# Output projection of five chunks as three products of two-part operands, in place of the fp32 product

## The chip, the cores and the metric

The kernel runs on one core of a Trainium2 chip. The metric is the device time of one execution in microseconds (us). A core has five engines that work side by side, each through its own list of instructions in order, and wait for one another by semaphores: TensorE (PE in the profile, its weight loads PEld), VectorE (DVE), ScalarE (ACT), GpSimd (POOL) and SyncE (SP, which here issues transfers).

## The reference, cut to what matters

The input x has 4 x 1024 tokens of 256 numbers. Three sublayers follow one another: a mixture of eight experts, causal attention with 16 heads of 16, and the same mixture of experts again. What the change touches is the output projection of the attention, the line with `w_proj`:

```python
x = x + 0.5 * _L0_ffn_ref(_layernorm(x), ...)
x = x + _L0_attn_ref(_layernorm(x), ...)       # below
x = x + 0.5 * _L0_ffn_ref(_layernorm(x), ...)
...
out = jnp.einsum('bhqk,bhkd->bhqd', attn, v)
out = out.transpose(0, 2, 1, 3).reshape(b, t, d)
proj = out @ w_proj + b_proj
x = proj + resid
mu = jnp.mean(x, axis=-1, keepdims=True)
var = jnp.var(x, axis=-1, keepdims=True)
return (x - mu) * jax.lax.rsqrt(var + EPS) * ln_gamma + ln_beta
```

All of it is float32.

## The kernel before

The 4096 tokens are 8 chunks of 512, and a chunk is 4 tiles of 128 tokens. The program has three stages: the first mixture of experts with the attention's inputs (names that begin with a_), the attention (b_), and a last stage that holds the output projection, the attention's norms and the second mixture of experts (c_). The last stage of chunks 0 to 2 is begun inside the end of the attention (the functions called `lead`); from then on it runs in slots. Slot c works on chunk c for its experts, and on later chunks for what must be ready by then:

- TensorE in slot c: the projection of chunk c+2 (`project`, L798; it is left out in slot 0), the bias product, then four tiles t of four expert products n (`experts`, L761), each product being six matmuls (`pair_product`, L349) into one of four PSUM banks, the ring. Between the tiles stand the transposes of chunk c+1 (`turn`, behind tile 0), its router product (behind tile 1), the transposes of its logits (behind tile 2), and the transpose of its mask (`turn_mask`, before the last product of tile 3).
- VectorE in slot c: `add_residual(c+2)` (it adds the projection from PSUM to the residual and takes the statistics), `combine(c, t)` for the four tiles (eight operations each, two for each expert product; they free the ring's banks), between them `split_lo(c+1)`, `attended(c+3)` (L1020, attention's numerator times the inverse of its denominator, 128x1024), `ranks(c+1)` (which experts a token takes; its last operation, L986, writes the mask), and `norm(c+2)` and `scale(c+2)` before `combine(c, 3)`.
- ScalarE in slot c: copies out of PSUM, `residual(c+3)`, and behind it `spread(c+2)` (the logarithm and exponential of the norm), `mask_out(c+1)` (L576) and `norm(c+2)`.
- GpSimd adds the two halves of a combined tile (L471) and does the wide additions of the norms (L485, L491, L497, L502).

The order within each engine is the order in which the code is written; there is no scheduler. The ring lets TensorE be four products ahead of VectorE:

```python
def ring_wait(pe, c, i):
    if i >= 4:
        pe.wait_ge(q.combined, at(32 * c + 2 * (i - 3) if exists(c) else 32 * NCH))
...
    else:
        pe.wait_ge(q.combined, at(32 * (c - 1) + 2 * (13 + i)))
```

So the first product of tile 1 waits until VectorE has combined the first product of tile 0 of the same chunk, and the first product of tile 0 waits until it has combined the first product of tile 3 of the chunk before.

`values` (L782) in the first stage has the form that the change brings into the last stage: 24 matmuls of `pair_product`, 256 columns wide, of operands in the type float32r.

Of the kernel before, what the change touches and what calls it, by code (L numbers as in the profile page):

```python
# [15 lines left out]
F32 = mybir.dt.float32  # L16
# [7 lines left out]
P = 128  # L24
# [6 lines left out]
CH = 512  # L31
# [132 lines left out]
def ffn(nc, s, ctx, a, first):  # L164
# [7 lines left out]
    def sb(name, shape, dt=F32):  # L172

        nonlocal offset
        here, size = offset, int(np.prod(shape[1:])) * (2 if dt == BF16 else 4)
        offset += -(-size // 32) * 32
        return nc.alloc_sbuf_tensor_at(f"{tag}_{name}", shape, dt, offset=here)
# [3 lines left out]
    def sem(name):  # L181
        every.append(ctx.enter_context(nc.semaphore(f"{tag}_{name}")))
        return every[-1]
# [25 lines left out]
    if first:  # L209
        q.st2, q.aggr2, q.std2, q.rstd2, q.norm2 = sem("st2"), sem("aggr2"), sem("std2"), sem("rstd2"), sem("norm2")  # L210
        q.xh2_ready, q.turned2, q.hi2_ready, q.lo2_ready = sem("xh2_ready"), sem("turned2"), sem("hi2_ready"), sem("lo2_ready")
        q.v_bank, q.v_ready, q.qk_bank = sem("v_bank"), sem("v_ready"), sem("qk_bank")
        q.qk_hi, q.qk_rest, q.qk_mid, q.qk_lo = sem("qk_hi"), sem("qk_rest"), sem("qk_mid"), sem("qk_lo")
        q.stored = s.qk_stored = [sem(f"stored{j}") for j in range(4)]
    else:
        q.num_loaded0, q.num_loaded1, q.att_ready = sem("num_loaded0"), sem("num_loaded1"), sem("att_ready")
        q.proj_bank, q.resid_ready, q.resid_bias, q.xa_ready = sem("proj_bank"), sem("resid_ready"), sem("resid_bias"), sem("xa_ready")
        q.st3, q.aggr3, q.std3, q.rstd3, q.norm3 = sem("st3"), sem("aggr3"), sem("std3"), sem("rstd3"), sem("norm3")
        q.y_ready, q.scaled, q.x_shifted, q.x2_ready = sem("y_ready"), sem("scaled"), sem("x_shifted"), sem("x2_ready")
        q.written = sem("written")  # L220
# [36 lines left out]
        xt.append([sb(f"xt1{n}", [P, DK, CH], F32R) for n in range(2)])  # L257
    ybias = [sb(f"ybias{pair}", [P, 2, D]) for pair in range(2)]
    acc = [[sb(f"acc{par}{n}", [P, D]) for n in range(2)] for par in range(2)]


    if first:
# [287 lines left out]
    def scalar(act):  # L550
# [85 lines left out]
        def norm3(m):  # L636
# [2 lines left out]
            act.wait_ge(q.scaled, at(m))  # L639
            normalize(act, yn, lambda t: xa[:, t, :], lambda t, n: ln3[:, t, n:n + 1], q.y_ready)  # L640

        def slot(c, par, nth):
            if exists(c):
                bias_out(c, 0)
            if first and exists(c - 1):
                norm2(c - 1)
            if not first and exists(c + 2):
                norm3(c + 2)
            if exists(c + 1):
                split_hi(c + 1, 1 - par)  # L650
                logits_out(c + 1)
            if exists(c):
                bias_out(c, 1)
            if first and exists(c - 1):
                split2(c - 1)
            if not first and exists(c + 3):
                residual(c + 3)
            if exists(c + 2):
                spread(c + 2)
            if exists(c + 1):  # L660
                mask_out(c + 1, 1 - par)
            if exists(c + 2):
                norm(c + 2)
            if first and exists(c - 1):
                v_out(c - 1)
                for j in (0, 2):
                    qk_hi(c - 1, j)
                    qk_hi(c - 1, j + 1)
                    qk_mid(c - 1, j)
                    qk_mid(c - 1, j + 1)  # L670

        if first:
            nc.scalar.preload_act_table_set("natural_log_exp_and_others")
            act.dma_start(wr_in[:], s.w_router).then_inc(q.router_in, 16)
            act.dma_start(be_in[:], s.b_experts).then_inc(q.bias_in, 16)
            act.dma_start(s.brouter[:], s.b_router).then_inc(q.router_in, 16)
            act.dma_start(wqk_in, s.w_qk).then_inc(q.qk_in, 16)
            act.dma_start(wv_in, s.w_v).then_inc(q.v_in, 16)
            act.wait_ge(q.consts, 3)
            act.activation(unused[:], s.eps[:, 0:1], ACT.Exp)  # L680
            weights_hi((0,))
            spread(0)
            norm(0)
            weights_hi(range(1, 5))
            split_hi(0, 0)
            weights_hi(range(5, WBANKS))
            act.wait_ge(q.router_in, 2 * 16)
            act.sem_inc(q.apart, 1)
            logits_out(0)
            act.wait_ge(q.qk_in, 16)  # L690
            act.activation(s.wqk[0][:], wqk_in, ACT.Copy).then_inc(q.wqk_hi, 1)
            act.wait_ge(q.v_in, 16)
            act.activation(s.wv[0][:], wv_in, ACT.Copy).then_inc(q.wqk_hi, 1)
            mask_out(0, 0)
            spread(1)
            norm(1)
        else:
            def lead(early, block):
                if (early, block) == (1, 6):
                    act.wait_ge(a.v_copied, at(NG))  # L700
                    residual(0)
                if (early, block) == (1, 10):
                    residual(1)
                if (early, block) == (0, 1):
                    spread3(0)
                if (early, block) == (0, 5):
                    spread(0)
                if (early, block) == (0, 7):
                    split_hi(0, 0)
                    spread3(1)  # L710
                if (early, block) == (0, 9):
                    logits_out(0)

            a.scalar(act, lead)
            spread(1)
            mask_out(0, 0)
            norm(1)
# [5 lines left out]
    def tensor(pe):  # L723
# [74 lines left out]
        def project(m, par, pairs=(0, 1)):  # L798
# [3 lines left out]
            for pair in pairs:  # L802
# [4 lines left out]
                                                s.wp[:, h, :], start=(h == 0), stop=(h == DK - 1))  # L807
                last.then_inc(q.proj_bank, 1)

        def slot(c, par, nth):  # L810
            if not first and exists(c + 2) and not (isinstance(c, int) and c == 0):
                project(c + 2, par)
            if first and isinstance(c, int) and c == 0:

                experts(0, 0, 0, (0, 1))
# [92 lines left out]
    def vector(dve):  # L908
# [108 lines left out]
        def attended(m, par, nth):  # L1017
            dve.wait_ge((q.num_loaded0, q.num_loaded1)[par], at(16 * 3 * (nth + 1)))
            dve.wait_ge(q.proj_bank, at(2 * (m - 1)))
            dve.tensor_tensor(att[par][:], num[par][:], rec[par][:], ALU.mult).then_inc(q.att_ready, 1)  # L1020

        def add_both(m):
            dve.wait_ge(q.resid_bias, at(m + 1))
            dve.wait_ge(q.y_ready, at(m))
            for pair in range(2):
                dve.wait_ge(q.proj_bank, at(2 * m + pair + 1))
                dve.tensor_tensor(xa[:, 2 * pair:2 * pair + 2, :], pt[pair][:].rearrange("p (t d) -> p t d", d=D),
                                  residb[:, 2 * pair:2 * pair + 2, :], ALU.add).then_inc(q.xa_ready, 1)
# [12 lines left out]
        def slot(c, par, nth):  # L1041
# [16 lines left out]
                combine(c, par, 2)  # L1058
            if exists(c + 1):
                ranks(c + 1, 1 - par)  # L1060
            if first and exists(c - 1):
                split2(c - 1)
            if first and not exists(c):
# [26 lines left out]
        else:  # L1090
# [45 lines left out]
                    scale(1)  # L1136

            a.vector(dve, lead)
        slots(dve, slot)

    f = Signals()
# [453 lines left out]
```

## Time and profile before

| what | value |
|---|---|
| median of 3 runs | 1014.38 us (1014.06 to 1014.91) |
| the profiled execution, its own time | 1014.85 us |
| its span, first to last instruction | 1013.1 us |
| TensorE busy | 966.1 us, 95% |
| VectorE busy | 832.3 us, 82% |
| ScalarE busy | 512.1 us, 51% |
| GpSimd busy | 264.6 us, 26% |
| granted TensorE clock, mean | 0.977 |
| slots of the last stage | 783.8 to 1013.1 us of the span |

Busy time is the time in which an engine's records say that it works; TensorE's matmuls overlap in the records, so that the time between two starts says more than the length of one. Idle time stands in brackets behind a row, with what ended it.

### The profile page before, as it was taken

The page shows a single profiled execution, that of the slowest core. Times are in us where ns is not written, and L with a number is a line of the kernel's source. Part 1 is how long each engine was busy: PE and PEld are TensorE (multiplying, and loading weights), DVE is VectorE, ACT ScalarE, POOL GpSimd, SP SyncE. Part 2 cuts the span into 40 slices and gives each one's busy share as a digit, 9 for nine tenths or more (in the row PEclk, how much of TensorE's full clock was granted, in tenths as well). Part 3 has the DMA queues.
Part 4 walks back from the last instruction along what each step waited for, and adds up shares of the span by engine and source line. Part 5 has one row for each costly group of instructions (what it writes and reads, how often), then busy time and mean ns, then how long its engine had stood idle before and what let it go on. Part 6 is the DMA issues. An engine that isn't in the chain of part 4 may idle for free.

```text
span 1013.1 us, 18108 instructions
## 1 busy us (share of the span) xinstructions
PE 966.1 (95%) x5602; PEld 574.2 (57%) x5602; DVE 832.3 (82%) x2444; ACT 512.1 (51%) x1053; POOL 264.6 (26%) x289
## 2 busy tenths in 40 slices
PE   6899999999897799999999999999997999999997
PEld 5678887888664233333333333333343777777776
DVE  6677676867665899999999999999768788888775
ACT  4235434442322377777777777777775333232210
POOL 1012202221423311212122222222343553434311
PEclk9999999999996799999999999999999999999999
DMA  7201101103103412223222323223320111110001
GB/s 228 81 1 63 58 6 62 63 28 98 63 23 102 127 47 68 71 65 73 70 68 74 76 77 76 77 75 76 81 70 13 43 63 63 62 61 22 1 21 42
DMA packets 55058, 64.27 MB, mean 63 GB/s; under 512 B 13776, under 2 KB 37312, under 8 KB 54976
## 3 DMA queue, kind: packets, MB, share of 16 engines
q1 hardware_dynamic: 54384, 62.47, 21.6%
q8 instruction: 40, 0.66, 0.3%
q10 hardware_dynamic: 592, 0.80, 0.2%
q14 instruction: 42, 0.34, 0.1%
HBM read 41.30 MB, written 21.23 MB: 62 GB/s over the span
## 4 chain that ended last, share of the span: by engine, by line
PE 86%; DVE 8%; issue 2%; ACT 2%; DMA 1%; POOL 1%; DVEq 0%; SPq 0%; POOLq 0%; ACTq 0%
PE bank L354 39%; PE bank L1507 14%; PE bank L1337 14%; PE bank L1491 13%; PE bank L806 2%; PE bank L346 2%; ACT b_probs L1470 1%; DVE bank L1364 1%; DMA v_all<-L_ffn_w_experts 1%; PE bank L757 1%; DVE a_acc L1005 1%; DVE b_neg L1368 1%; DVE c_acc L1005 1%; DVE c_eq L978 1%; DVE a_st L309 1%
## 5 line engine op out<-in xcount | busy, mean ns | idle before, releaser
L1470 ACT ACTIVATE b_probs<-bank 128x512 f32<-128x512 f32 (+1 forms) x608 | 302.3, 587 | 121.0 <-PE bank L1491 120.5
L1364 DVE CUSTOM_DVE_ANT_0 bank<-bank,b_below 128x384 f32<-128x384 f32 (+3 forms) x512 | 234.9, 516 | 7.8 <-PE bank L1337 6.3
L1337 PE MATMUL bank<-b_ks,b_qs 96*128 96x512 bf16 (+3 forms) x768 | 226.3, 337 | 15.3 <-DVE b_neg L1368 5.4
L1491 PE MATMUL bank<-b_qs,b_ks 99*128 99x512 bf16 (+3 forms) x768 | 214.6, 331 | 4.5 <-ACT b_probs L1470 4.3
L354 PE MATMUL bank<-we,a_xt 128*128 128x512 f32 x768 | 190.6, 402 | 1.7 <-DVE a_acc L1005 1.7
L354 PE MATMUL bank<-we,c_xt 128*128 128x512 f32 x768 | 187.7, 399 | 0.5 <-DVE c_acc L1005 0.5
L1444 POOL TENSOR_SCALAR_AFFINE_SELECT b_probs<-b_probs 128x512 f32<-128x512 f32 x128 | 83.9, 656 | 333.7 <-ACT b_probs L1470 319.6
L1368 DVE TENSOR_REDUCE b_neg<-bank 128x1 f32<-128x512 f32 x256 | 160.6, 679 | 3.0 <-PE bank L1337 1.6
L354 PEld LDWEIGHTS bank<-we,a_xt 128*128 128x128 f32 x768 | 143.0, 191 | 30.7 <-DVE a_acc L1005 1.7
L354 PEld LDWEIGHTS bank<-we,c_xt 128*128 128x128 f32 x768 | 141.8, 188 | 31.8 <-DVE c_acc L1005 0.8
L1507 PE MATMUL bank<-b_probs,b_vs 128*32 128x512 f32 (+3 forms) x1536 | 155.7, 500 | 0.9 <-POOL b_probs L1444 0.9
L1337 PEld LDWEIGHTS bank<-b_ks,b_qs 96*128 96x128 bf16 x768 | 68.0, 98 | 124.6 <-DVE b_neg L1364 51.0
L1491 PEld LDWEIGHTS bank<-b_qs,b_ks 99*128 99x128 bf16 x768 | 66.1, 98 | 108.7 <-ACT b_probs L1470 70.6
L1005 DVE SCALAR_TENSOR_TENSOR c_acc<-bank,c_mask,c_acc 128x256 f32<-128x256 f32 x192 | 81.6, 477 | 22.8 <-PE bank L354 22.0
L1005 DVE SCALAR_TENSOR_TENSOR a_acc<-bank,a_mask,a_acc 128x256 f32<-128x256 f32 x192 | 81.2, 477 | 18.4 <-PE bank L354 17.9
L471 POOL TENSOR_TENSOR xs<-a_acc,a_acc 128x256 f32<-128x256 f32 (+1 forms) x32 | 24.9, 778 | 221.2 <-DVE a_acc L1005 221.2
L1364 DVE DVE_READ_ACCUMULATOR2_ANT b_neg<- 128x1 f32 x512 | 69.6, 136 | 0.0
L1507 PEld LDWEIGHTS bank<-b_probs,b_vs 128*32 128x32 f32 x1536 | 35.3, 109 | 56.9 <-ACT b_probs L1470 36.1
L471 POOL TENSOR_TENSOR xs<-c_acc,c_acc 128x256 f32<-128x256 f32 (+1 forms) x32 | 29.0, 906 | 100.9 <-DVE c_acc L1005 100.9
L1015 DVE TENSOR_TENSOR a_rest<-bank,a_part 128x512 f32<-128x512 f32 x32 | 22.1, 691 | 32.8 <-ACT a_part L620 28.2
L354 PE MATMUL bank<-a_xt2r,a_wqk 128*128 128x512 f32 x192 | 46.4, 397 | 0.0
L325 ACT ACTIVATE a_std<-a_mv,eps 128x4 f32<-128x4 f32 x16 | 4.8, 298 | 76.6 <-DVE a_mv L314 76.6
(133 smaller groups left out, 912.1 us busy)
## 6 DMA issues: line engine op xcount, KB each, us to landing
b_qs<-q_parts SPq DMA_DIRECT2D x96, 128.0 KB, 3.0
b_ks<-k_parts SPq DMA_DIRECT2D x96, 128.0 KB, 3.1
q_parts<-a_part SPq DMA_DIRECT2D x16, 384.0 KB, 2.7
k_parts<-a_part SPq DMA_DIRECT2D x16, 384.0 KB, 2.7
att_num<-b_oev SPq DMA_DIRECT2D x64, 64.0 KB, 2.2
c_num<-att_num SPq DMA_DIRECT2D x8, 512.0 KB
c_rec<-att_rec SPq DMA_DIRECT2D x16, 256.0 KB
out<-xs SPq DMA_DIRECT2D x8, 512.0 KB, 3.1
```

The lines of the kernel that those rows point to most:

```text
L346: last = nc.tensor.transpose(dst[h][:, t * P:(t + 1) * P], src[:, t, h * P:(h + 1) * P], s.ident[:])
L354: last = nc.tensor.matmul(out_, wa if x_moves else xa_, xa_ if x_moves else wa, start=(n == 0), stop=(n == len(steps) - 1))
L471: pool.tensor_tensor(s.xs[:, row(c, t), :].rearrange("p a d -> p (a d)"), acc[t % 2][0][:], acc[t % 2][1][:], ALU.add).then_inc(q.x_ready, 1)
L1005: dve.scalar_tensor_tensor(out=dst[:], in0=ring[n][:, i * D:(i + 1) * D], scalar=mask[par][:, t, 2 * n + i:2 * n + i + 1], in1=base, op0=A ...
L1015: dve.tensor_tensor(rest[j % 2][:], ring[j][:], part[j][:, 0, :], ALU.subtract).then_inc(q.qk_rest, 1)
L1337: last = nc.tensor.matmul(ms[bank][:, a * width:(a + 1) * width], qs[g.u][0:ROWS, c, i * P:(i + 1) * P], ks[g.u][0:ROWS, c, lo:lo + width] ...
L1364: last = dve.tensor_tensor_reduce(part, part, below[:, CH - width:CH], -1.0, 3.0e38, ALU.add, ALU.min, dst[:, a, :])
L1368: dve.tensor_reduce(dst, ms[bank][:, 0:len(heads) * width].rearrange("p (h w) -> p h w", w=width), AX.X, ALU.max, negate=True).then_inc(mr ...
L1444: pool.affine_select(out=part, in_=part, compare_op=ALU.is_ge, fill=0.0, base=0, pattern=[[0, GH], [1, P]], channel_multiplier=-1).then_in ...
L1470: act.activation(probs[b % 4][:, heads[0]:heads[0] + hp, 0:width], es[exp_bank(g, unit)][:, 0:hp * width].rearrange("p (h w) -> p h w", w= ...
L1491: last = nc.tensor.matmul(es[exp_bank(g, unit)][:, a * width:(a + 1) * width], ks[g.u][:, c, j * P:(j + 1) * P], qs[g.u][:, c, first_q:fir ...
L1507: last = nc.tensor.matmul(os_[half][SLOT * c:SLOT * (c + 1), start:CH], vs[g.n % 2][:, j, c, :], probs[b % 4][:, c, 0:width], start=(j == ...
```

## The change

Chunks 3 to 7 (those projected in slots 1 to 5) take another form of projection. `w_proj` is split once into two parts of the type float32r: ScalarE copies it (`wpr[0]`), VectorE subtracts that copy from it (`wpr[1]`). The attended values of each of the five chunks are split in the same way: `attended_hi` on ScalarE behind `residual(c+3)`, `attended_lo` on VectorE behind `ranks(c+1)` and before `norm(c+2)`. TensorE then adds three products (first part by first part, first by second, second by first) for each of the two halves of the contraction, 24 matmuls for a chunk in place of 16 fp32 ones. Chunks 0 to 2 keep the fp32 product. No transfer is added or moved.

```diff
+        q.wp_hi, q.wp_lo, q.att_hi, q.att_lo = sem("wp_hi"), sem("wp_lo"), sem("att_hi"), sem("att_lo")
...
+    if not first:
+        wpr = [sb(f"wpr{n}", [P, DK, D], F32R) for n in range(2)]
+        attr = [sb(f"attr{n}", [P, DK, CH], F32R) for n in range(2)]
...
+        def attended_hi(m, par):
+            act.wait_ge(q.att_ready, at(m + 1))
+            act.wait_ge(q.proj_bank, at(2 * m))
+            act.activation(attr[0][:], att[par][:], ACT.Copy).then_inc(q.att_hi, 1)
...
             if not first and exists(c + 3):
                 residual(c + 3)
+                attended_hi(c + 3, 1 - par)
             if exists(c + 2):
                 spread(c + 2)
...
             a.scalar(act, lead)
+            act.activation(wpr[0][:], s.wp[:], ACT.Copy).then_inc(q.wp_hi, 1)
             spread(1)
...
+        def project_parts(m):
+            pe.wait_ge(q.wp_lo, at(1))
+            pe.wait_ge(q.att_lo, at(m - 2))
+            pe.wait_ge(q.lo_ready, at(2 * (m - 1)))
+            pe.wait_ge(q.xa_ready, at(2 * m))
+            for pair in range(2):
+                for i in range(2):
+                    t = 2 * pair + i
+                    last = pair_product(pt[pair][:, i * D:(i + 1) * D], wpr, slice(0, D), attr, slice(t * P, (t + 1) * P),
+                                        False)
+                last.then_inc(q.proj_bank, 1)
...
             if not first and exists(c + 2) and not (isinstance(c, int) and c == 0):
-                project(c + 2, par)
+                project_parts(c + 2)
...
+        def attended_lo(m, par):
+            dve.wait_ge(q.att_hi, at(m - 2))
+            dve.tensor_tensor(attr[1][:], att[par][:], attr[0][:].bitcast(F32), ALU.subtract).then_inc(q.att_lo, 1)
...
             if exists(c + 1):
                 ranks(c + 1, 1 - par)
+            if not first and exists(c + 3):
+                attended_lo(c + 3, 1 - par)
...
             a.vector(dve, lead)
+            dve.wait_ge(q.wp_hi, at(1))
+            dve.tensor_tensor(wpr[1][:], s.wp[:], wpr[0][:].bitcast(F32), ALU.subtract).then_inc(q.wp_lo, 1)
```

Two places show it in the order of the instructions. The first is VectorE in a slot of the loop, from the last operation of `ranks` on (`c_mask` is the mask, `c_attr_170` and `c_attr_171` the first and the second part of the attended values, `c_st` and `c_mv` the norm's statistics). Before:

```order
L986 TENSOR_SCALAR c_mask_156<-c_rank 128x4x24
L309 ISA
L309 BN_STATS c_st<-xs 128x6
L309 ISA
L309 BN_STATS c_st<-xs 128x6
```

And in the changed kernel, whose lines are numbered otherwise:

```order
L1010 TENSOR_SCALAR c_mask_156<-c_rank 128x4x24
L1048 TENSOR_TENSOR c_attr_171<-c_att_131,c_attr_170 128x1024
L314 ISA
L314 BN_STATS c_st<-xs 128x6
L314 ISA
```

One subtraction of 128x1024 stands between the mask and the statistics, and all that VectorE does later in the slot stands behind it. The second place is TensorE at the turn of a slot, from the last expert product of chunk c to the bias product of chunk c+1. Before:

```order
L354 MATMUL bank<-we,c_xt_160 128x512
L799 REGISTER_ALU
L806 MATMUL bank<-wp,c_att_131 128x256 x8
L757 MATMUL bank<-bias_rows,c_mask_t_158 128x256 x2
```

(The list shows the fp32 matmuls as eight; the profile has 16 for a chunk.) And now, with the first three and the last three of 24:

```order
L359 MATMUL bank<-we,c_xt_160 128x512
L359 MATMUL bank<-c_wpr_168,c_attr_170 128x256
L359 MATMUL bank<-c_wpr_168,c_attr_171 128x256
L359 MATMUL bank<-c_wpr_169,c_attr_170 128x256
...
L359 MATMUL bank<-c_wpr_168,c_attr_170 128x256
L359 MATMUL bank<-c_wpr_168,c_attr_171 128x256
L359 MATMUL bank<-c_wpr_169,c_attr_170 128x256
L769 MATMUL bank<-bias_rows,c_mask_t_158 128x256 x2
```

Nothing else moves on TensorE.

## Rows read from the trace of the kernel before

**Rows 1.** Page: TensorE's busy time; chain that ended last, by line.

```profile
PE 966.1 (95%) x5602; PEld 574.2 (57%) x5602; DVE 832.3 (82%) x2444; ACT 512.1 (51%) x1053; POOL 264.6 (26%) x289
PE bank L354 39%; PE bank L1507 14%; PE bank L1337 14%; PE bank L1491 13%; PE bank L806 2%; PE bank L346 2%; ACT b_probs L1470 1%; DVE bank L1364 1%; DMA v_all<-L_ffn_w_experts 1%; PE bank L757 1%; DVE a_acc L1005 1%; DVE b_neg L1368 1%; DVE c_acc L1005 1%; DVE c_eq L978 1%; DVE a_st L309 1%
```

**Rows 2.** Windows from tile 1 to tile 1: us, busy of PE, PEld, DVE, ACT, POOL.

```profile
790.40:819.92 29.52, 29.34 (x138) 22.81 (x137) 23.81 (x61) 9.82 (x22) 13.33 (x8) 1.00 0.22 72
909.26:938.91 29.65, 29.36 (x138) 22.87 (x137) 24.62 (x63) 9.99 (x24) 13.39 (x8) 1.00 0.10 35
```

**Rows 3.** Timeline of TensorE, 867 to 881 us: start, us, operation, [idle before].

```profile
867.77 0.23 PE L750 MATMUL bank<-ident_b,c_mask 128*128 128x128 bf16 x1 [0.29 <-DVE c_mask L986]
...
869.36 3.62 PE L806 MATMUL bank<-wp,c_att 128*128 128x256 f32 x16
872.82 0.38 PE L757 MATMUL bank<-bias_rows,c_mask_t 128*128 128x256 bf16 x2
872.96 5.83 PE L354 MATMUL bank<-we,c_xt 128*128 128x512 f32 x24
...
879.41 5.83 PE L354 MATMUL bank<-we,c_xt 128*128 128x512 f32 x24
```

**Rows 4.** Timeline of VectorE, the same stretch.

```profile
867.51 0.21 DVE L986 TENSOR_SCALAR c_mask<-c_rank 128x96 bf16<-128x96 f32 x1
...
871.05 0.48 DVE L1005 SCALAR_TENSOR_TENSOR c_acc<-bank,c_mask,xs 128x256 f32<-128x256 f32 x1
...
878.58 0.47 DVE L1005 SCALAR_TENSOR_TENSOR c_acc<-bank,c_mask,xs 128x256 f32<-128x256 f32 x1
```

**Rows 5.** Timeline of VectorE and TensorE at the start of slot 1's tile 1.

```profile
818.78 0.47 DVE L1005 SCALAR_TENSOR_TENSOR c_acc<-bank,c_mask,xs 128x256 f32<-128x256 f32 x1
...
819.92 5.83 PE L354 MATMUL bank<-we,c_xt 128*128 128x512 f32 x24
```

**Rows 6.** Timeline of the slot without a projection, where TensorE waits for VectorE.

```profile
958.87 0.47 DVE L1005 SCALAR_TENSOR_TENSOR c_acc<-bank,c_mask,xs 128x256 f32<-128x256 f32 x1
...
959.40 5.86 PE L354 MATMUL bank<-we,c_xt 128*128 128x512 f32 x24 [0.53 <-DVE c_acc L1005]
```

**Rows 7.** Timeline of TensorE, first stage: the 24 matmuls of values.

```profile
147.40 3.01 PE L354 MATMUL bank<-a_wv,a_xt2r 128*128 128x256 f32 x24
150.25 5.82 PE L354 MATMUL bank<-a_xt2r,a_wqk 128*128 128x512 f32 x24
```

**Rows 8.** Timeline of VectorE, first stage: subtractions that split 1024 and 512 columns.

```profile
20.89 1.22 DVE L1085 TENSOR_TENSOR a_wqk<-v_all,a_wqk 128x1024 fp32r<-128x1024 f32 x1
22.03 0.68 DVE L1087 TENSOR_TENSOR a_wv<-v_all,a_wv 128x512 fp32r<-128x512 f32 x1
```

**Rows 9.** One line's instructions: ScalarE's copy of 1024 columns (ns, min/median/max).

```profile
L691 ACT ACTIVATE a_wqk<-v_all x1: 1041/1041/1041, 17.8 to 17.8; 128x1024 fp32r<-128x1024 f32 x1
```

**Rows 10.** Timeline of ScalarE, around the mask of the same slot.

```profile
869.79 0.30 ACT L325 ACTIVATE c_std<-c_mv,eps 128x4 f32<-128x4 f32 x1 [9.68 <-DVE c_mv L314]
...
870.23 0.26 ACT L576 ACTIVATE c_mask_t<-bank 128x128 bf16<-128x128 bf16 x1
```

**Rows 11.** Timeline of VectorE: first combination of tile 2, and its idle time.

```profile
888.53 0.48 DVE L1005 SCALAR_TENSOR_TENSOR c_acc<-bank,c_mask,c_ybias 128x256 f32<-128x256 f32 x1 [1.16 <-PE bank L354]
```

**Rows 12.** Timeline of VectorE and TensorE at the start of slot 0's tile 1.

```profile
788.48 0.48 DVE L1005 SCALAR_TENSOR_TENSOR c_acc<-bank,c_mask,xs 128x256 f32<-128x256 f32 x1
...
790.40 5.83 PE L354 MATMUL bank<-we,c_xt 128*128 128x512 f32 x24
```

**Rows 13.** Timeline of GpSimd: the first work behind the mask at 867.72.

```profile
874.14 0.75 POOL L471 TENSOR_TENSOR xs<-c_acc,c_acc 128x256 f32 x1 [8.20 <-DVE c_acc L1005]
```

**Rows 14.** Timeline: a VectorE product beside a GpSimd addition.

```profile
777.11 2.58 DVE L976 TENSOR_TENSOR c_wins<-c_eq,before 128x256 f32<-128x256 f32 x1
...
776.88 2.53 POOL L485 TENSOR_TENSOR c_residb<-c_resid,bproj 128x1024 f32<-128x1024 f32 x1
```

**Rows 15.** Timeline of VectorE: the same product, GpSimd idle.

```profile
954.21 0.41 DVE L976 TENSOR_TENSOR c_wins<-c_eq,before 128x256 f32<-128x256 f32 x1
```

## Prediction

> **What bounds the kernel now.** I read the page first: TensorE is busy for 95% of the span, and the chain that ended last lies on it for most of its length; the fp32 projection L806 has 2% of that chain [rows 1]. From the page alone the change is a gain, since it takes time from TensorE. But the share is an average over three stages, so I went to the last stage by windows, cut where the experts of tile 1 begin, once for each slot. From slot 0's tile 1 to slot 5's there are five such periods, each 29.5 to 29.9 us, with 29.3 to 29.4 us of TensorE in them and 23.8 to 24.7 us of VectorE [rows 2]; the first and the last are shown. TensorE is nearly full, VectorE has some 5 us to spare. What has to be asked is whether the spare time lies where the change puts its work.
>
> So next the timelines of both engines side by side at the turn of a slot. TensorE waits 0.29 us for the mask, starts the mask's transpose at 867.77 and the last product behind it, then the projection at 869.36, the bias product at 872.82, tile 0 at 872.96 and tile 1 at 879.41 [rows 3]. VectorE ends the mask at 867.51 + 0.21 = 867.72, ends the first pair of tile 3 at 871.05 + 0.48 = 871.53, and the first pair of tile 0 at 878.58 + 0.47 = 879.05 [rows 4]. Tile 1 on TensorE may not start before that last time (the ring has four banks). It started at 879.41, so VectorE was only 0.36 us ahead. At slot 1's tile 1 it was 819.92 - 819.25 = 0.67 us ahead [rows 5]. Over the five turns the lead is 0.67, 0.52, 0.36, 0.54 and 0.65 us, 2.74 us in sum; the largest and the smallest are shown.
>
> The two engines thus run in a ring with hardly any slack: tile 1 on TensorE, the router, tile 2, then VectorE's ranks and mask (VectorE is waiting for products in tile 2, 1.16 us before its first operation there [rows 11], so the mask comes at a fixed time behind TensorE's tile 1), then VectorE without a real pause from the mask to tile 0's first pair, 867.72 to 879.05, 11.33 us, and then TensorE's tile 1 again. The 5 us that VectorE has to spare lie in tiles 1 and 2, and none of it lies on that stretch, except the lead above.
>
> **The change part by part.**
>
> TensorE's saving. The 16 fp32 matmuls take 872.82 - 869.36 = 3.46 us, 216 ns each [rows 3]. The new form stands in the first stage, same widths, type and helper: 24 matmuls in 150.25 - 147.40 = 2.85 us, 119 ns each [rows 7]. That is 0.61 us less for a chunk, 3.05 us for five. The Trainium skill has another price for the old form: FP8 and Floating Point Precision, TensorE Precision Notes, says that a true fp32 product takes four passes through the array. At one column a cycle and 2.4 GHz that makes 427 ns for 256 columns, 6.8 us for a chunk, and an estimated saving of 4 us for each in place of 0.61. The measured 216 ns does not agree with that, and the measurement decides.
>
> VectorE's subtraction, in slots 0 to 4, right behind the mask. The same form (128x1024, fp32r from f32) took 1.22 us, and the next operation started 22.03 - 20.89 = 1.14 us behind its start [rows 8]; 1.14 us is what it adds to the queue. Behind it stand the norm's statistics, the scale, tile 3's combination, the addition of the residual and its statistics, and tile 0's combination; all are 1.14 us later. In a loop slot it needs one more wait whose bound is a register; that I take at nothing, because such a wait can be read while the operation before it runs, and at most at 0.1 us (0.4 us for four slots).
>
> Who waits for what is late. (a) The bias product needs the mask's copy on ScalarE, which ends at 870.23 + 0.26 = 870.49 [rows 10] and stands behind the norm's logarithm and exponential; it is now at 871.63, and TensorE comes there at 872.82 - 0.61 = 872.21. Hidden, by 0.58 us. (b) Tile 0's first product waits for tile 3's first pair: 871.53 + 1.14 = 872.67, TensorE comes at 872.96 - 0.61 = 872.35. A wait of about 0.4 us, where there was none. (c) Tile 1 follows 6.45 us behind tile 0's start on TensorE (879.41 - 872.96), at 872.73 + 6.45 = 879.18; VectorE's pair ends at 879.05 + 1.14 = 880.19. How fast TensorE starts when it does wait there is shown by the slot that has no projection: pair's end 958.87 + 0.47 = 959.34, start 959.40, 0.06 us [rows 6]. So tile 1 starts at 880.25, 0.84 us later than before, with a wait of 1.07 us. The 0.61 us saved is spent in these two waits.
>
> For one turn the time grows by 1.14 + 0.06 less the lead, and over five turns by 5 x 1.20 - 2.74 = 3.26 us. The saving of 3.05 us isn't subtracted: it lies on a branch that now waits for VectorE. Does the loss come back later? From slot 5 on VectorE has no subtraction and TensorE's own work again sets the pace; a start that is 3.26 us late stays late, as tiles there wait for TensorE only.
>
> ScalarE's copy, 1024 columns, 1.04 us [rows 9], stands behind the residual, in front of the norm's logarithm, before which ScalarE was idle for 9.68 us [rows 10]. Nothing; without that cover it would delay the mask's copy and cost up to 0.5 us a slot beyond (a)'s margin. VectorE asks for the copy only behind the mask, several us later, so no wait there. The projection itself asks for the second part: it ends about 867.72 + 1.14 = 868.86, TensorE begins the projection at 869.36. Nothing, with 0.5 us of margin.
>
> The split of the weights, once, at the start of the slots: ScalarE 0.6 us while it is idle; VectorE 0.68 us, 0.60 in the queue [rows 8], in front of chunk 2's residual. There VectorE led by 790.40 - (788.48 + 0.48) = 1.44 us [rows 12], so 0.8 us is left, and this costs nothing. That lead is why slot 0's turn isn't counted.
>
> The sum: 1014.85 + 3.3 = 1018.1 us for an execution like the profiled one. It lay 0.47 us above the median, so for the median 1014.38 + 3.3 = 1017.7 us, 0.32% slower.
>
> **Rivals.**
>
> *The subtraction is hidden, and TensorE's gain arrives.* Faster: 1014.38 - 3.05 = 1011.3 us. It wants the subtraction to cost less than the lead: the turn breaks even with no change where it adds 2.74 / 5 - 0.06 = 0.49 us, and the full gain needs VectorE to arrive 0.61 us earlier than that, which is below nothing. So even a subtraction of half the time gives no gain; what would is that the lead is larger than I read it, for example if the recorded ends of VectorE are late or TensorE's start at 879.41 waits on something that I don't see. Against it stands the slot without a projection, in which the same wait shows openly [rows 6]. Chance 0.07.
>
> *Partly hidden.* The leads are read from one execution, and idle stretches on VectorE between the mask and tile 0 may shrink when their releaser (ScalarE) is early. Between -2 and +2 us, no change that can be measured, some 1015 us. Chance 0.09.
>
> *The subtraction meets GpSimd.* An operation of VectorE with two inputs from SBUF beside a GpSimd addition ran for 2.58 us, until that addition (776.88 + 2.53) was over; the same product took 0.41 us with GpSimd idle [rows 14, 15]. The new subtraction has two such inputs. If a wide addition ran at its start, it would pay up to 2.17 us more in each slot: 5 x 2.17 = 10.9 us, 1028.5 us. Against it: GpSimd was idle for 8.20 us up to 874.14, hence since 865.9, 1.7 us before the mask's end [rows 13], and what it does before that is timed by TensorE's tile 2, as the mask is. It decides only if GpSimd comes 1.7 us later relative to the mask. Chance 0.04. The Trainium skill, SBUF — State Buffer, section SBUF: two separate sides, states it as a rule that speaks against such an operation: VectorE with two SBUF inputs and GpSimd hold a shared pair of ports by turns, each for a whole instruction. By that rule, the trace agrees [rows 14, 15].
>
> *More than the subtraction.* The register wait, a projection that waits for its second part, and a longer path through ScalarE add up to 1 us a slot: up to 1023 us. Chance 0.05, the far end of what my case gives.
>
> **How the numbers follow.** My own case, 0.75, reaches from 1016.4 (each turn 0.25 us cheaper) to 1019.4 us (0.1 us of register wait, leads 0.2 us smaller). A measurement of this kernel can tell 0.2%, 2 us, from no change. For 8 in 10 I take in part of the hidden and of the expensive side: 1015.6 to 1020.4 us. Slower by over 2 us (above 1016.4): my case nearly whole and the two expensive ones, 0.82. Within 2 us: 0.10. Faster: 0.08.
>
> **What would show it.** TensorE's 24 new matmuls take about 2.85 us at the turn of slots 1 to 5. The subtraction takes 1.2 us behind each mask, and the statistics start 1.14 us later behind the mask than before. New idle time of TensorE for VectorE's combination at tile 0 (0.4 us) and tile 1 (0.6 to 1.1 us) of chunks 1 to 5, some 6 us together. The five periods [rows 2] take 30.2 to 30.5 us each; up to 790 us and from slot 5's tile 1 on, all durations are as before. It is wrong if these waits are missing and the periods fall to 29 us, or if the subtraction runs beyond 2 us.

## The result and the profile after

The changed kernel takes 1017.54 us (median of 20 runs), the kernel before 1014.42 us beside it (20 runs); the ratio is 1.0022, with a 95% interval of 1.0015 to 1.0030. The medians lie 3.1 us apart and the ratio says 2.2 us (1.5 to 3.0): 3 of the 20 executions of the changed kernel, 1013.4 to 1013.7 us at a mean granted clock of 0.981 where the others have 0.975 to 0.978, were some 4 us shorter than the rest, and with them left out the means lie 3.0 us apart. What makes those three different isn't settled. The profiled execution took 1018.04 us with a span of 1016.3 us, 3.2 us more than before in both.

The page has TensorE where it was, at 95% [rows 1], and the chain by line shows what came in: VectorE's statistics and combination and the residual's addition have 2%, 2% and 1%.

```profile
PE 966.6 (95%) x5642; PEld 574.3 (57%) x5642; DVE 837.4 (82%) x2450; ACT 516.7 (51%) x1059; POOL 265.5 (26%) x289
...
PE bank L359 36%; PE bank L1539 14%; PE bank L1369 14%; PE bank L1523 13%; PE bank L351 2%; DVE c_st L314 2%; DVE c_acc L1029 2%; ACT b_probs L1502 1%; DMA v_all<-L_ffn_w_experts 1%; PE bank L818 1%; DVE bank L1396 1%; DVE c_xa L1055 1%; DVE b_neg L1400 1%; DVE a_acc L1029 1%; PE bank L769 1%
```

The windows from one start of tile 1's experts to the next, in the columns of [rows 2]; here are the first and the last of the five and their sum:

```profile
790.51:820.61 30.10, 29.21 (x144) 22.72 (x143) 25.65 (x64) 11.07 (x25) 13.68 (x8) 1.00 0.16 53
...
911.94:942.06 30.12, 29.32 (x143) 22.78 (x144) 25.47 (x64) 10.73 (x24) 13.43 (x8) 1.00 0.11 40
sum 151.55, PE 146.55 PEld 113.84 DVE 127.81 ACT 54.26 POOL 67.41; mean PE 29.31 PEld 22.77 DVE 25.56 ACT 10.85 POOL 13.48
```

The five are 30.10, 30.44, 30.47, 30.42 and 30.12 us long. Before they ran from 790.40 to 938.91, 148.51 us; now from 790.51 to 942.06, 151.55 us. The 3.04 us between these are nearly all of the 3.2 us that the span grew, so these five turns are the place. Their sum, called the five periods below, is also the finest measure of the experiments: it leaves out the first two stages, whose time differs from run to run.

The same turn of a slot as in [rows 3], on TensorE:

```profile
869.17 0.23 PE L762 MATMUL bank<-ident_b,c_mask 128*128 128x128 bf16 x1 [0.29 <-DVE c_mask L1010]
869.26 1.65 PE L359 MATMUL bank<-we,c_xt 128*128 128x512 f32 x6
870.74 3.03 PE L359 MATMUL bank<-c_wpr,c_attr 128*128 128x256 f32 x24
873.61 0.39 PE L769 MATMUL bank<-bias_rows,c_mask_t 128*128 128x256 bf16 x2
873.99 5.86 PE L359 MATMUL bank<-we,c_xt 128*128 128x512 f32 x24
879.68 1.04 PE L351 MATMUL bank<-ident,c_xh 128*128 128x128 f32 x8
881.52 5.84 PE L359 MATMUL bank<-we,c_xt 128*128 128x512 f32 x24 [0.80 <-DVE c_acc L1029]
```

The 24 matmuls take 873.61 - 870.74 = 2.87 us. From the transposes' start to tile 1 there are 1.84 us, of which 1.05 are new: an undisturbed turn has 0.79 there (876.57 - 875.78 in the last kernel of the experiments). And on VectorE, the rows that answer to [rows 4]:

```profile
868.91 0.21 DVE L1010 TENSOR_SCALAR c_mask<-c_rank 128x96 bf16<-128x96 f32 x1
869.03 1.22 DVE L1048 TENSOR_TENSOR c_attr<-c_att,c_attr 128x1024 fp32r<-128x1024 f32 x1
870.17 1.40 DVE L314 BATCH_NORM_STATS2 c_st<-xs 128x6 f32 x4
...
873.46 0.47 DVE L1029 SCALAR_TENSOR_TENSOR c_acc<-bank,c_mask,xs 128x256 f32<-128x256 f32 x1
...
880.99 0.47 DVE L1029 SCALAR_TENSOR_TENSOR c_acc<-bank,c_mask,xs 128x256 f32<-128x256 f32 x1
```

The subtraction takes 1.22 us, the statistics begin 1.14 us behind its start, and tile 0's first pair ends at 881.46, 0.06 us before TensorE's tile 1. In the list of TensorE's waits between 790 and 945 us the first line is new, five such waits with 3.3 us of recorded idle time; the second, for the mask, stood there before with the same 1.7 us:

```profile
PE bank L359 <- DVE c_acc L1029: 3.3, 5, 0.8
PE bank L762 <- DVE c_mask L1010: 1.7, 5, 0.5
```

### The profile page after: what moved, and what is told of

The parts are those of the page before. It is cut to its first block, busy times and chain, and to the rows that moved or that the text cites. A ratio compares the mean times of both kernels' runs of the same rounds, so it can differ in the third digit from the quotient of the medians.

```text
span 1016.3 us, 18218 instructions
## 1 busy us (share of the span) xinstructions
PE 966.6 (95%) x5642; PEld 574.3 (57%) x5642; DVE 837.4 (82%) x2450; ACT 516.7 (51%) x1059; POOL 265.5 (26%) x289
## 4 chain that ended last, share of the span: by engine, by line
PE 80%; DVE 11%; issue 4%; ACT 3%; DMA 1%; POOL 1%; DVEq 1%; SPq 0%; POOLq 0%; ACTq 0%
PE bank L359 36%; PE bank L1539 14%; PE bank L1369 14%; PE bank L1523 13%; PE bank L351 2%; DVE c_st L314 2%; DVE c_acc L1029 2%; ACT b_probs L1502 1%; DMA v_all<-L_ffn_w_experts 1%; PE bank L818 1%; DVE bank L1396 1%; DVE c_xa L1055 1%; DVE b_neg L1400 1%; DVE a_acc L1029 1%; PE bank L769 1%
## 5 line engine op out<-in xcount | busy, mean ns | idle before, releaser
L330 ACT ACTIVATE c_std<-c_mv,eps 128x4 f32<-128x4 f32 x16 | 4.8, 303 | 81.4 <-DVE c_mv L319 81.4
```

## The experiments

The theory: a slot's turn is a ring, TensorE from tile 1 to the mask and VectorE's queue from the mask to tile 0's first pair; the subtraction stands in it and TensorE's saving does not. The main rival: the loss is more work for a VectorE that is 82% busy, or the new matmuls or ScalarE's copy cost something. All ratios are to the kernel before, of runs made beside it; the five periods are those of the one execution of each kernel that was profiled.

| kernel | median us | ratio, 95% interval | five periods us |
|---|---|---|---|
| before | 1014.42 | 1 | 148.51 |
| changed | 1017.54 | 1.0022 (1.0015 to 1.0030) | 151.55 |
| no_lo | 1012.83 | 0.9981 (0.9972 to 0.9990) | 146.39 |
| split_fp32 | 1017.7 | 1.0030 (1.0017 to 1.0042) | 151.56 |
| lo_half | 1015.57 | 1.0007 (0.9993 to 1.0020) | 148.83 |
| lo_twice | 1023.36 | 1.0089 (1.0075 to 1.0103) | 157.30 |
| hi_thrice | 1017.85 | 1.0033 (1.0017 to 1.0049) | 151.52 |
| lo_moved | 1017.5 | 1.0031 (1.0019 to 1.0043) | 153.90 |
| att_early | 1017.08 | 1.0024 (1.0012 to 1.0035) | 150.62 |
| resid_after | 1012.22 | 0.9973 (0.9957 to 0.9989) | 146.21 |
| resid_before | 1011.84 | 0.9972 (0.9954 to 0.9991) | 145.89 |
| lo_gpsimd | 1009.53 | 0.9951 (0.9933 to 0.9969) | 142.85 |

### Without the subtraction (no_lo)

```diff
             if not first and exists(c + 3):
-                attended_lo(c + 3, 1 - par)
...
-            pe.wait_ge(q.att_lo, at(m - 2))
+            pe.wait_ge(q.att_hi, at(m - 2))
...
+            dve.tensor_tensor(attr[1][:], num[0][:], num[0][:], ALU.subtract)   # once
```

> The changed kernel without VectorE's subtraction of the attended values; the second part is filled once with zeros, so that TensorE has its 24 matmuls but the projection lacks the small part. ScalarE's copy stays. Theory: as the run with the subtraction moved, five periods of some 146.1 us and some 1012.0 us, since nothing but the lead is left. Rival (the new matmuls, or ScalarE's copy, cost something too): periods above 148.5 us, a time not under that of before.

Five periods of 146.39 us, 2.12 us below the kernel before and 0.3 us above the forecast. The matmuls and the copy cost nothing, and TensorE's saving arrives as far as VectorE's lead lets it.

### The fp32 projection with both splits in place (split_fp32)

```diff
-                project_parts(c + 2)
+                project(c + 2, par)
```

> Both splits stay where the changed kernel has them, but TensorE keeps the fp32 projection of 16 matmuls for all chunks, and nobody reads the parts. Theory (the saving on TensorE lies on a branch that waits for VectorE): the same time as the changed kernel, five periods of some 151.5 us and 1017.5 us, although TensorE works 3 us longer. Rival (loss and saving add up): 3 us above the changed kernel, periods of 154.6 us, 1020.6 us.

151.56 us against 151.55 us of the changed kernel. This is the plainest result: with the subtraction in its place it makes no difference to the time whether TensorE's projection takes 3.46 or 2.87 us, and the whole loss comes without a single new matmul. Loss and saving do not add up.

### Half the subtraction, and twice (lo_half, lo_twice)

```diff
-            dve.tensor_tensor(attr[1][:], att[par][:], attr[0][:].bitcast(F32), ALU.subtract).then_inc(q.att_lo, 1)
+            dve.tensor_tensor(attr[1][:, 0, :], att[par][:, 0, :], attr[0][:, 0, :].bitcast(F32), ALU.subtract).then_inc(q.att_lo, 1)
```

```diff
+            dve.tensor_tensor(spare[:], att[par][:], attr[0][:].bitcast(F32), ALU.subtract).then_inc(q.apart, 1)
             dve.tensor_tensor(attr[1][:], att[par][:], attr[0][:].bitcast(F32), ALU.subtract).then_inc(q.att_lo, 1)
```

> The changed kernel with only one of the two halves of the attended values subtracted, 128x512 in place of 128x1024; the other half's second part is filled once with zeros, so that the projection lacks it. ScalarE's copy and the 24 matmuls stay. The 128x512 subtraction takes 0.60 us of VectorE's queue in the trace of the kernel before. Theory (a turn grows by what the subtraction adds, plus 0.06 us, less a lead of 0.55 us on the mean): 5 x 0.66 - 2.74 = 0.6 us more than before, five periods of 149.1 us, 1015.0 us, with 2.7 us less than the changed kernel. Rival (the loss is a fixed cost of the added instruction and its wait): as the changed kernel, 151.5 us.

> The changed kernel with the subtraction of the attended values done twice in the same place, the first time into a spare tile. Theory: the lead and TensorE's own saving are used up, so each of the five turns grows by the whole 1.14 us, 5.7 us: five periods of 157.2 us, 1023.2 us. The projection then also has to wait for its second part, which ends 2.3 us behind the mask while TensorE comes there 1.6 us behind it, but that wait is covered by the one at tile 1. Rival (VectorE's spare 5 us of a slot take part of it): an increase well under 5.7 us.

(lo_half leaves the second part of the other half at zero.) With nothing, half, one and two subtractions the five periods are 146.39, 148.83, 151.55 and 157.30 us. From half to one they grow by 2.72 us (5 x 0.54), from one to two by 5.75 us (5 x 1.15, the 1.14 us that one adds to the queue): above the lead all that VectorE's queue grows by counts, and a fixed cost of the instruction is ruled out. From nothing to half only 2.44 us arrive of 3.0 (5 x 0.60), since part of it is still inside the lead. In lo_twice TensorE waits for the second part itself as well, as was forecast:

```profile
875.82 0.38 PE L360 MATMUL bank<-c_wpr,c_attr 128*128 128x256 f32 x1 [0.78 <-DVE c_attr L1050]
```

That wait adds nothing to the sum: the growth of 5.75 us is VectorE's alone.

### ScalarE's copy three times (hi_thrice)

```diff
+            act.activation(spare[0][:], att[par][:], ACT.Copy)
+            act.activation(spare[1][:], att[par][:], ACT.Copy)
             act.activation(attr[0][:], att[par][:], ACT.Copy).then_inc(q.att_hi, 1)
```

> The changed kernel with ScalarE's copy of the attended values made three times, twice into spare tiles, 2.1 us more of ScalarE in each of five slots. Theory (it stands in front of 9.7 us in which ScalarE is idle, and VectorE asks for it 7 us later): five periods of 151.5 us as in the changed kernel, 1017.5 us. Rival (the copy delays the norm's logarithm and the mask's copy, and part of the measured loss is ScalarE's): several us more.

151.52 us, as the changed kernel. ScalarE's rows show why: the last copy ends at 863.88, and the logarithm behind it waits 7.87 us more for VectorE.

```profile
862.84 1.04 ACT L653 ACTIVATE c_attr<-c_att 128x1024 fp32r<-128x1024 f32 x1
871.76 0.30 ACT L331 ACTIVATE c_std<-c_mv,eps 128x4 f32<-128x4 f32 x1 [7.87 <-DVE c_mv L320]
```

### The splits moved to where VectorE has time (lo_moved, att_early): a miss

```diff
             if exists(c + 1):
                 split_hi(c + 1, 1 - par)
+            if not first and exists(c + 3):
+                attended_hi(c + 3, 1 - par)
...
-                attended_hi(c + 3, 1 - par)
...
+            if not first and exists(c + 3):
+                attended(c + 3, 1 - par, nth + 1 + par)
             if exists(c):
                 combine(c, par, 1)
             if not first and exists(c + 3):
-                attended(c + 3, 1 - par, nth + 1 + par)
+                attended_lo(c + 3, 1 - par)
...
-            if not first and exists(c + 3):
-                attended_lo(c + 3, 1 - par)
```

> All of the change is kept, but the splitting of the attended values is put where VectorE and ScalarE have time: VectorE makes the attended values before the combination of tile 1 in place of behind it, ScalarE copies the first part behind the split of the transposes, and VectorE subtracts behind the combination of tile 1. Nothing new stands between the mask and tile 0. Theory (VectorE's queue from the mask to tile 0's first pair sets the pace, and the subtraction there is the whole loss): TensorE's 0.61 us a turn arrives as far as VectorE's lead allows, which is the lead less 0.06 us: 0.61, 0.46, 0.30, 0.48, 0.59, 2.4 us in sum. The five periods fall from 148.5 us of before to some 146.1, and the time to some 1012.0 us. Rival (the loss comes from the extra work on VectorE wherever it stands, since it is 83% busy): no better than the changed kernel, 1017.5 us.

I forecast 146.1 us and 1012.0 us, and got 153.90 us in the profiled execution and a median of 1017.5 us. That execution, 1020.2 us, was the longest of six, and four others lie at 1017.1 to 1017.5 us. Outside the five periods it is no longer than the kernel before (864.6 us of the span in both), so my estimate for the periods of a typical execution is 1017.5 - (1020.2 - 153.90) = 151.2 us: as slow as the changed kernel, and not slower. As it stands, that would speak for the rival (extra work hurts wherever it is). The trace shows a more particular cause. VectorE's multiplication and GpSimd's wide addition, in the same stretch:

```profile
855.87 3.23 DVE L1046 TENSOR_TENSOR c_att<-c_num,c_rec 128x1024 f32<-128x1024 f32 x1 [0.49 <-DMA c_rec<-att_rec]
```

```profile
855.62 2.40 POOL L507 TENSOR_TENSOR xs<-c_yg,c_xb 128x1024 f32 x1 [0.21 <-POOL c_yg L502]
```

The multiplication took 3.23 us and not the 1.21 us of the kernel before: it began while GpSimd's addition ran, to 858.02, and ended 1.08 us behind it. It is what [rows 14] show. In front of it VectorE waited for the transfer of the inverse denominators too, for which the old place had been late enough. Then tile 1's combination came late, and TensorE waited 0.59 us and more at tile 2. Late too were the logits on ScalarE, the residual, GpSimd's two additions, and so the first operation of the ranks, a comparison with two inputs from SBUF that took 2.09 us where it takes 0.42 alone; TensorE's wait for the mask rose from 0.29 to 0.92 us in this slot, and from 1.7 to 4.8 us over the five:

```profile
871.46 0.23 PE L764 MATMUL bank<-ident_b,c_mask 128*128 128x128 bf16 x1 [0.92 <-DVE c_mask L1012]
```

To see how much is due to the multiplication's place alone, the next kernel has only that edit, made to the kernel before:

> The kernel before with one edit: VectorE makes the attended values of chunk c+3 in front of the combination of tile 1, not behind it. No split, no new instruction. It takes one edit out of the run with the moved subtraction, which was as slow as the changed kernel against my forecast. Theory: at that place GpSimd runs its wide addition into xs, and the multiplication, with two inputs from SBUF, waits until it is over: 3.2 us in place of 1.2 us in at least four of five slots. Tile 1's combination then starts 3 us or more later, TensorE's tile 2 waits for it, and the five periods are 150 to 152 us, 1016 to 1018 us. Rival (the moved run was slow for ScalarE's copy in front of the logits, which pushed the residual and GpSimd's additions back): the multiplication is still slow, but VectorE catches up, and the periods are 148.5 us.

Five periods of 150.62 us, 2.1 us above the kernel before, in the range of the first theory. By the medians, each against the kernel before beside it, this one edit costs 2.3 us and lo_moved 2.7 us; so most of lo_moved's typical time over the kernel before is there without any split. In its longer profiled execution the periods are 5.4 us above those of before, and what the two split operations (ScalarE's copy in front of the logits, and the subtraction) add to that I have not taken apart. The waits of VectorE show why they could not be free there: between 790 and 940 us it waited 15.3 us for TensorE's products in the kernel before, 5.2 us in att_early and 1.0 us in lo_moved. Its spare time was used up, by the slow multiplication, the 2.9 us of waits for transfers and the moved subtraction, so in this much the rival was right. Part of the theory was too simple: the multiplication was slow in four of five slots (2.4 to 3.4 us), but in the first it waited 3.88 us for its transfer and not for GpSimd. That first period grew most, by 0.90 us of the 2.11 (30.42 for 29.52 us); so the collision with GpSimd accounts for at most 1.2 us, and that wait for 0.9 us.

```profile
796.02 1.23 DVE L1020 TENSOR_TENSOR c_att<-c_num,c_rec 128x1024 f32<-128x1024 f32 x1 [3.88 <-DMA c_rec<-att_rec]
...
883.92 3.35 DVE L1020 TENSOR_TENSOR c_att<-c_num,c_rec 128x1024 f32<-128x1024 f32 x1 [0.37 <-DMA c_rec<-att_rec]
```

### The ring shortened elsewhere (resid_after, resid_before)

The collision can also be taken out of the ring. In the kernel before, the first operation of the ranks ran 1.45 us beside GpSimd's addition L491; with that addition over it takes 0.42 us (the third line is from resid_before). ScalarE's residual starts those additions, and it stood behind a wait of 5.7 us.

```profile
863.89 1.45 DVE L973 TENSOR_TENSOR c_eq<-c_logits 128x256 f32<-128x256 f32 x1
862.64 2.42 POOL L491 TENSOR_TENSOR c_xb<-xs,beta 128x1024 f32<-128x1024 f32 x1
```

```profile
863.27 0.42 DVE L974 TENSOR_TENSOR c_eq<-c_logits 128x256 f32<-128x256 f32 x1
```

```diff
                 split_hi(c + 1, 1 - par)
+            if not first and exists(c + 3):
+                residual(c + 3)
+            if exists(c + 1):
                 logits_out(c + 1)
...
-                residual(c + 3)
```

> The changed kernel with ScalarE's residual(c+3) moved in front of the logits' copy, where ScalarE waits 5.7 us for the router. GpSimd's two wide additions, which wait for it, then start some 2 us earlier and are over before VectorE's ranks, whose first product ran 1.45 us in place of 0.42 us while they ran. Theory (VectorE's queue is the loop, and anything that shortens it from TensorE's tile 1 to the mask shows in full): each turn 1.0 us shorter, five periods of 146.4 us, 1012.4 us, and the first product of ranks at 0.42 us. Rival (the change lost its time in something other than this ring): no difference from the changed kernel.

> The kernel before, fp32 projection and no split, with the same move of residual(c+3). Theory: the mask comes 1.0 us earlier, and TensorE's waits for it (0.18, 0.46, 0.29, 0.46, 0.29 us) vanish; the rest goes into VectorE's lead. Five periods of 146.8 us, 1012.7 us. So the changed kernel with the same move, at 146.4 us, would be hardly better: the two-part projection would have nothing to give even then. Rival (GpSimd's additions meet another operation of VectorE at their new place): at or above 148.5 us.

The changed kernel falls by 5.34 us to 146.21 us (forecast 146.4). The one before falls by 2.62 us to 145.89 us (forecast 146.8). In both the first operation of the ranks takes 0.42 us, and TensorE's waits for the mask are gone. This is a third way to the same reading: what is taken from VectorE's part of the ring shows in full where the subtraction makes that part the longer one (5 x 1.07), and only partly where TensorE's part is (2.62). And it again leaves nothing for the two-part projection: with it the five periods are 0.32 us longer than without, and by the ratios (0.9973 and 0.9972) the two can't be told apart.

For resid_before I was 0.9 us off. I had taken TensorE's recorded idle time before the mask's transpose, 1.68 us over five turns, for all that it loses there. Start to start, from tile 3's first matmul to the mask's transpose:

```profile
862.41 4.45 PE L354 MATMUL bank<-we,c_xt 128*128 128x512 f32 x18
866.71 0.23 PE L751 MATMUL bank<-ident_b,c_mask 128*128 128x128 bf16 x1
```

4.30 us here. In the kernel before:

```profile
863.03 4.45 PE L354 MATMUL bank<-we,c_xt 128*128 128x512 f32 x18
```

867.77 - 863.03 = 4.74 us, where the record shows 0.29 us of idle time [rows 3]. The matmuls' records overlap by about 0.15 us here, and a wait shows as idle only beyond that.

### The subtraction on GpSimd (lo_gpsimd): faster than both

```diff
                 if exists(c + 3):
                     add_bias(c + 3)
-                    shift_x(c + 3)
+                    attended_lo(c + 3, 1 - par)     # now GpSimd's
                 add_tiles(c, (2, 3))
+                if exists(c + 3):
+                    shift_x(c + 3)
```

(with the early residual of resid_after, and VectorE's subtraction taken out)

> The changed kernel with residual(c+3) early on ScalarE, as in the run before this one of that kind, and the subtraction of the attended values on GpSimd in place of VectorE, in the stretch where GpSimd did the addition L491 (shift_x), which moves behind the last tile's sum, where GpSimd is idle. Theory (TensorE's 0.6 us a turn is worth its full price as soon as VectorE's queue from the mask on is free of the subtraction): VectorE leads tile 1 by 0.9 us in the kernel before with the early residual, more than the 0.61 us by which TensorE now comes earlier, so five turns are each 0.6 us shorter than its 145.9 us: 142.9 us, and some 1009 us. The subtraction takes 2.4 us on GpSimd, as L485 does. Rival (GpSimd's operations at the new places hold a VectorE operation with two inputs from SBUF for up to 2 us): at or above 145.9 us.

142.85 us, forecast 142.9; 1009.53 us, 0.49% under the kernel before. GpSimd's rows of one slot:

```profile
856.53 2.41 POOL L490 TENSOR_TENSOR c_residb<-c_resid,bproj 128x1024 f32<-128x1024 f32 x1
858.91 2.38 POOL L502 TENSOR_TENSOR c_attr<-c_att,c_attr 128x1024 fp32r<-128x1024 f32 x1
...
872.08 2.43 POOL L496 TENSOR_TENSOR c_xb<-xs,beta 128x1024 f32<-128x1024 f32 x1
```

The subtraction takes 2.38 us, twice VectorE's time, and costs nothing: it is over at 861.29, before the ranks' first comparison with two inputs from SBUF starts on VectorE at 862.15. TensorE is busy through every period:

```profile
876.57:905.14 28.57, 28.57 (x147) 22.70 (x145) 23.44 (x64) 10.89 (x24) 15.77 (x9) 1.00 0.16 55
...
sum 142.85, PE 142.85 PEld 113.49 DVE 116.66 ACT 54.50 POOL 78.91; mean PE 28.57 PEld 22.70 DVE 23.33 ACT 10.90 POOL 15.78
```

Against resid_before, which in these periods has no wait of TensorE for VectorE left either, that is 3.04 us less, 0.61 us a turn: the saving of the new matmuls at full price.

## Why the prediction was right

Direction, mechanism and size held: 1017.7 us was forecast for the median and 1017.54 us measured, 3.26 us for the profiled execution and 3.2 us found. That the median came within 0.2 us is in part luck: the ratio of all runs says 2.2 us, and its interval ends at 3.0, below the forecast. By its own steps:

- *TensorE's saving, 0.61 us for a chunk.* It measured 3.46 - 2.87 = 0.59 us, and 0.61 us a turn where it could arrive. My reading of the other price was wrong, though it changed no term of the sum. I took the profile's 16 records for 16 matmuls. The kernel issues 8 for a chunk (4 tiles times 2 halves of the contraction, and the list in the section on the change has x8), and the profile shows each as two records, so that one fp32 matmul of 256 columns takes 3.46 / 8 = 0.43 us. The Trainium skill's four passes (FP8 and Floating Point Precision, TensorE Precision Notes) give an estimate of 427 ns for each of the 8 at one column a cycle and 2.4 GHz, 3.4 us a chunk, and the trace agrees (granted clock 1.00 in these periods): there was never a saving of 4 us to be had.
- *The subtraction adds 1.14 us to VectorE's queue.* Behind its start the next operation came 1.14 us later, in every slot. What the turn grew by was less in the slots of the loop: mask to statistics, start to start, was 867.75 - 867.51 = 0.24 us [rows 4] (the second time is in the row below) and is 870.17 - 868.91 = 1.26 us, 1.02 us more; in slot 0 it is 1.13 us more. In the loop something of 0.1 us stands in front of the statistics that the subtraction now covers, perhaps the reading of an address; no run shows what it is. I had allowed for up to 0.1 us of the other sign, for the register of the new wait, and none of it is there: from mask to statistics there are 1.26 us in slot 0 as in the loop.

```profile
867.75 1.41 DVE L309 BATCH_NORM_STATS2 c_st<-xs 128x6 f32 x4
```

- *The leads, 2.74 us in sum.* The five turns grew by 0.58, 0.61, 0.81, 0.57 and 0.47 us; the sum of the terms gave 0.53, 0.68, 0.84, 0.66 and 0.55 us. The turn with the smallest lead grew most, as it had to. Two of the five periods, 30.10 and 30.12 us, lie just under the 30.2 to 30.5 that I gave as a sign. VectorE's stretch from the mask to tile 0's first pair, which I called without a real pause, has 1.7 us in which VectorE does nothing, 1.3 of them in the norms, where ScalarE works between two operations of VectorE; this did not shrink (0.68 and 0.60 us for 0.67 and 0.60), which is why nothing was partly hidden.
- *The waits.* Tile 1: 1.07 us forecast, 1.05 us found. Tile 0: 0.4 us forecast; from the bias product to tile 0 there are 0.38 us in place of 0.14, so 0.24 us: the pair came 1.02 and not 1.14 us later with respect to the mask. Too short to stand as idle time in the record. Start to start the two waits come to 5.6 us over the five turns, near the 6 us forecast, of which the record shows 3.3 us as idle.
- *The branches costed at nothing.* ScalarE's copy (hi_thrice), the wait for the second part (lo_twice) and the weights' split cost nothing or nearly so. The last was closer than I had it: VectorE led slot 0's tile 1 by 1.44 us before and by 0.06 us now, and tile 1 starts at 790.51, 0.11 us later. The split took 0.6 us of that lead; in front of it VectorE waited 1.71 us for a transfer, and 0.77 us before, which I had not looked at.
- *The rivals.* That the subtraction is hidden fell with lo_half: even at half its length there is no gain over before. The collision with GpSimd did not happen at the place the change gives it, but it slowed lo_moved and att_early, where I had forgotten it for my own edit. In all five slots the subtraction took 1.22 us. The Trainium skill's rule (SBUF — State Buffer, SBUF: two separate sides) that one of the two holds the shared ports for a whole instruction agrees with the 3.23 us.
- *The range.* Its upper end for my own case, 1019.4 us, is added up wrongly: 1017.7 with 0.4 us of register waits and five leads smaller by 0.2 us is 1019.1 us. Nothing rests on it.

## What to carry to other kernels

Before work is moved off the busiest engine, look for the ring that paces the loop, and ask at which point of the other engine's queue the new work stands: here VectorE had 5 us to spare in 30, and 1.14 us in the wrong place cost more than TensorE had saved. Measure the lead (when the waited-for operation ends, against when the waiter starts); up to it new work is free, beyond it all of it counts, and the saving on the waiting side is worth nothing. When an operation with two inputs from SBUF is moved on VectorE, look at what GpSimd does at the new time, not only at VectorE's idle time.

## What the hardware showed that I had not expected

- A wait of TensorE costs more than the idle time in the record: 0.29 us recorded and 0.44 us lost at the mask, 0.80 us recorded and 1.05 us lost before tile 1, nothing recorded and 0.24 us lost before tile 0.
- The profile shows an fp32 matmul as two records. One of 256 columns takes 432 ns from start to start, in records of 216 ns, and one of float32r some 120 ns: three products of two-part operands (24 matmuls, 2.87 us) are 17% cheaper than one fp32 product (8 matmuls, 3.46 us).
- GpSimd's wide additions stood in the ring of the kernel before already, by holding one VectorE comparison for 1.0 us a slot; one line moved on ScalarE took 0.28% (0.09 to 0.46%) off the whole time.
